# A graph network and a mixture of experts: the experts' second layer with tokens on partitions at once

## The chip, the cores and the metric

One core of a Trainium2 chip runs the whole kernel. The metric is device time in microseconds of one execution; lower is better.

## What is computed

The input is 16 graphs of 512 nodes with 128 features, and a 512 x 512 adjacency mask for each. The first block adds to every node the result of a small graph network; the second adds to every node a mixture of 8 experts, of which each node takes the best 2. Cut to what matters here:

```python
    # block 1, per graph: convolutions, message passing, GRU gates
    x = x + gnn(layernorm(x), adj)
    # block 2, on every node of every graph
    xn = layernorm(layernorm(x)) * gamma + beta
    logits = xn @ Wr + br                      # 8 experts
    top_vals, top_idx = top_k(logits, 2)
    w_full = softmax(top_vals) put at top_idx, 0 elsewhere
    for e in range(8):
        h = gelu(xn @ W1[e] + b1[e])           # 128 -> 256
        y_e = h @ W2[e] + b2[e]                # 256 -> 128
        y = y + y_e * w_full[..., e]
    x = x + y
```

## The kernel before, in words

Every engine runs one long list of instructions, written out by hand; semaphores join them. The order of these lists is what sets the order of the work.

**The graphs.** `iteration(g)` (one for each engine: TensorE L622, ScalarE L838, VectorE L1359, POOL L1001, the DMA queue SP L447) does the graph network of graph g, finishes graph d = g - 1 (residual sum, statistics, routing) and, from graph 4 on (`FIRST`), four expert tiles beside it. The products of the graph network are exact float32 from three passes in a reduced type (`product`, L527: high by high, low by high, high by low). Graph steps named in the prediction: `conv_sum` and `conv_diff` (the 17-tap convolution), `dist` (four products whose exponentials become the adjacency weights), the products with the hidden weights that begin with `HH + 1` (L687 to L691), the message product L706, the gates (L710 to L729), `nn` (L923) on ScalarE. `dist(3)` at L675 writes the PSUM bank M and so waits for `msg_done`, the copy `msg_t` on ScalarE (L882). Behind it on ScalarE come four exponentials (L885) and the gelu of tile 1.

**Routing and tiles.** Graphs 0 to 13 are routed: each normalized row goes by indirect DMA (POOL, `rows_to_experts`) to the region of its two experts in DRAM, with its weights for all 8 experts. A tile is 256 such rows of one expert. SP loads the rows (`xt`) and the expert's weights (`w_t`, one block per expert in DRAM: first layer high and low, second layer, biases, a one-hot row) through 8 buffers. The last two graphs are dense: all experts on all their rows, without routing. There are 66 tiles, 48 of them streamed beside graphs 4 to 15, and in the tail behind the graphs 18 tiles and 32 dense halves, in the order of `items` (L379).

**One tile.** TensorE turns the rows so that features lie on partitions (`turn`), ScalarE and VectorE split them into high and low (`turned`, `tile_lo`), TensorE makes the first layer (`hidden`), ScalarE the gelu (`gelu`). Then the part that is changed. `second` (L591) gives the result with features on partitions; `results` (L805) on ScalarE adds the bias, one value per partition, into `yT`; `back` (L600) turns it by two transposes so that tokens lie on partitions; `weigh` (L1303) on VectorE multiplies by each row's weight for the tile's expert; POOL adds the rows into `out` by indirect DMA (`add`, L970, and `last_add`, L989), each waiting until the adds before it have landed (in the tail: those of the experts before it). The row weight, `own_weight` (L1290), is made on VectorE: rows' weights times the one-hot row, then a sum. For a dense half `dense_weigh` (L1311) multiplies and adds into the graph's rows `x1_d` on VectorE.

**Where the tile steps stand.** TensorE: `tile_a(j)` (hidden of tile j, turn of the next, back of the one before) and `tile_b(j)` (second). ScalarE, in this order: results of the last tile of the graph before, `tile_gelu(0)`, `both` (L878), `tile_results(0)`, `msg_t`, the exponentials, `tile_gelu(1)`, `tile_turned(2)`, `normalized_rows` (L819), `tile_results(1)`, `xnT`, ..., `nm_h` (L908), `tile_results(2)`, `gap_weights` (L825, a tanh that VectorE's `place` waits for), the gates' tanh, ..., `nn`. VectorE: `operands_lo`, `residual_sum` with its statistics (L1397), `tile_own(0)` (L1398), the roots and tables of the routing, `tile_weigh(0)`, `normalize_x`, the four products with the mask (L1414), `tile_split(2)`, `tile_own(1)`, ..., `tile_split(3)`, `tile_own(2)`, `place`, ..., `tile_weigh(2)`, L1463, `tile_own(3)`, ..., `tile_weigh(3)`, `differences`.

**SP.** For each graph it stores the rows of graph d, loads `x_ln`, then `adj` of the next graph (L468, 1 MB, as soon as the mask products are done), `x_res`, and then, once the rows of the routing have landed, the four tiles of the next graph.

```python
                if g == FIRST - 1:
                    sp.wait_ge(w12_stored, 16)
                    sp.wait_ge(pads_stored, 16)
                if FIRST - 1 <= g < GRAPHS - 1:
                    chosen = [choice(g % 2, j) for j in range(SLOTS)]
                    for i in range(2):
                        sp.wait_ge(rows_out[i], 16 * NT * TOP * ((g - i) // 2))
                    for j in range(SLOTS):
                        next_loads(j)
```

## Time and profile before

| | |
|---|---|
| median of 3 runs | 658.0 us (655.03 to 658.53) |
| the profiled execution | 653.8 us, its span 652.0 us |
| TensorE busy | 614.0 us (94%) |
| TensorE loading weights (beside it) | 530.6 us (81%) |
| VectorE busy | 499.2 us (77%) |
| ScalarE busy | 418.1 us (64%) |
| POOL busy | 359.1 us (55%) |
| mean granted clock of TensorE | 0.985 |

The span is the time from the first to the last instruction; what the run's time has beyond it lies around the program. Busy shares are means over the whole span. A matmul in full float32 appears as two records, each with a weight load of its own; a busy time counts a record until its result is out, so records overlap, and the chain of waits shows their true distance. The chain of waits follows the work that ended last backwards, from each step to what released it; an idle time of an engine comes with the event that ended it.

### The profile page before, as it was taken

The numbers are of one execution on the slowest core, as the hardware profiler recorded it, in microseconds if no ns is written. First come the engines' busy times: TensorE is split into PE (matmuls) and PEld (weight loads), VectorE is DVE, ScalarE is ACT, GpSimd is POOL, SyncE is SP. The second block draws the span as 40 slices with busy tenths as digits, with TensorE's granted clock in tenths as the row PEclk, the third lists the DMA queues.
The fourth block names the chain that finished last, engine by engine and source line by source line (L and its number), as shares of the span: only waits on it lengthen the run. The fifth ranks groups of instructions, "written<-read, shape, count | busy, mean of one in ns | idle before, by whom it ended". The sixth has DMA issues, their size and how long they took to land.

```text
span 652.0 us, 12860 instructions
## 1 busy us (share of the span) xinstructions
PE 614.0 (94%) x3784; PEld 530.6 (81%) x3784; DVE 499.2 (77%) x2050; ACT 418.1 (64%) x824; POOL 359.1 (55%) x274
## 2 busy tenths in 40 slices
PE   2899999989999999999999999999999978999994
PEld 2779788777989897988888888888897957899993
DVE  6968898988888888888889888988787864544331
ACT  3644646494858575858586767676685745677772
POOL 3200405244854566575758685858485854545676
PEclk9998999999999999999999999999999998899998
DMA  8427241628398746465565655565647676993353
GB/s 299 145 80 266 73 123 53 204 89 247 65 291 250 191 115 186 128 165 153 138 171 141 165 149 161 153 166 144 165 110 192 167 167 157 236 252 46 53 94 46
DMA packets 93413, 101.01 MB, mean 155 GB/s; under 512 B 7664, under 2 KB 71920, under 8 KB 93040
## 3 DMA queue, kind: packets, MB, share of 16 engines
q1 hardware_dynamic: 70752, 83.27, 40.0%
q0 software_dynamic: 22592, 16.92, 17.0%
q8 instruction: 31, 0.51, 0.3%
q14 instruction: 38, 0.31, 0.2%
HBM read 75.85 MB, written 30.51 MB: 163 GB/s over the span
## 4 chain that ended last, share of the span: by engine, by line
PE 66%; DMA 7%; issue 7%; POOL 6%; ACT 6%; DVE 5%; POOLq 1%; another core or an unknown queue 0%; SPq 0%; DVEq 0%; ACTq 0%
PE G L706 9%; PE C L528 7%; PE C L530 7%; PE C L529 7%; POOL out L997 5%; PE G L528 5%; PE Y L596 5%; PE G L530 5%; PE G L529 5%; DMA out<-adj,ids 4%; PE M L534 2%; PE C L700 2%; PE Y L604 2%; DMA out<-ex,ids 2%; PE G L559 2%
## 5 line engine op out<-in xcount | busy, mean ns | idle before, releaser
L976 POOL DMA_INDIRECT out<-y_t,xt x96 | 159.4, 1660 | 121.7 <-DMA out<-y_t,xt 82.0
L1011 POOL DMA_INDIRECT routed<-row,at_u x112 | 130.6, 1166 | 116.2 <-DVE at_u L1208 83.6
L528 PE MATMUL C<-cv_h,w_hi 128*128 128x256 f32 (+1 forms) x432 | 131.6, 305 | 2.7 <-ACT tz L878 1.3
L530 PE MATMUL C<-cv_h,w_lo 128*128 128x256 f32 (+1 forms) x432 | 125.0, 289 | 0.0
L529 PE MATMUL C<-cv_l,w_hi 128*128 128x256 f32 (+1 forms) x432 | 124.9, 289 | 0.0
L528 PEld LDWEIGHTS C<-cv_h,w_hi 128*128 128x128 f32 x432 | 83.3, 193 | 5.7 <-issue 2.5
L529 PEld LDWEIGHTS C<-cv_l,w_hi 128*128 128x128 f32 x432 | 83.1, 192 | 1.3
L530 PEld LDWEIGHTS C<-cv_h,w_lo 128*128 128x128 f32 x432 | 83.0, 192 | 0.6
L596 PE MATMUL Y<-ge,w_t 128*128 128x256 f32 x228 | 59.8, 385 | 2.1 <-ACT ge L801 1.3
L706 PE MATMUL G<-ex,msg_t 128*128 128x512 f32 x128 | 58.9, 603 | 0.3 <-ACT gh L899 0.3
L596 PEld LDWEIGHTS Y<-ge,w_t 128*128 128x128 f32 x228 | 41.3, 192 | 12.7 <-issue 6.7
L801 ACT ACTIVATE ge<-H,w_t 128x256 f32<-128x256 f32 x114 | 47.9, 473 | 3.6 <-PE H L573 2.7
L908 ACT CAST cv_h<-G 128x512 fp32r<-128x512 f32 x16 | 9.4, 588 | 51.4 <-PE G L706 41.6
L706 PEld LDWEIGHTS G<-ex,msg_t 128*128 128x128 f32 x128 | 23.1, 190 | 23.5 <-issue 23.0
L528 PE MATMUL G<-xlT_h,w_hi 128*128 128x512 f32 x96 | 40.0, 417 | 1.5 <-DVE xlT_l L1139 1.5
L1414 DVE TENSOR_TENSOR ex<-ex,adj 128x512 f32<-128x512 f32 x64 | 39.8, 679 | 0.0
L530 PE MATMUL G<-xlT_h,w_lo 128*128 128x512 f32 x96 | 38.6, 402 | 0.0
L529 PE MATMUL G<-xlT_l,w_hi 128*128 128x512 f32 x96 | 38.3, 399 | 0.0
L571 PE MATMUL H<-xT_h,w_t 128*128 128x256 f32 x114 | 36.9, 323 | 0.0
L604 PE MATMUL Y<-cst,yT 128*128 128x128 f32 x146 | 29.9, 287 | 5.6 <-ACT yT L809 4.1
L1287 DVE TENSOR_TENSOR xT_l<-H,xT_h 128x256 fp32r<-128x256 f32 x57 | 23.9, 418 | 12.0 <-ACT xT_h L794 9.4
L809 ACT ACTIVATE yT<-Y,w_t 128x256 f32<-128x256 f32 x57 | 27.0, 474 | 9.3 <-PE Y L596 6.7
(264 smaller groups left out, 1703.3 us busy)
## 6 DMA issues: line engine op xcount, KB each, us to landing
w_t<-w_all SPq DMA_DIRECT2D x66, 392.0 KB, 3.5
adj<-adj_t SPq DMA_DIRECT2D x16, 1024.0 KB
xt<-routed SPq DMA_DIRECT2D x66, 144.0 KB
x_ln<-x SPq DMA_DIRECT2D x16, 256.0 KB
x_res<-x SPq DMA_DIRECT2D x16, 256.0 KB
wd<-w_all SPq DMA_DIRECT2D x10, 392.0 KB
out<-x SPq DMA_DIRECT2D x15, 256.0 KB
w_all<-w_s SPq DMA_DIRECT2D x1, 3136.0 KB, 11.4
```

The lines of the kernel that those rows point to most:

```text
L528: pe.matmul(psum, hi(w), rhs_h, start=start, stop=False)
L529: pe.matmul(psum, hi(w), rhs_l, start=False, stop=False)
L530: return pe.matmul(psum, lo(w), rhs_h, start=False, stop=stop)
L571: pe.matmul(half, w[:, h * P:(h + 1) * P], x_h, start=True, stop=False)
L596: last = pe.matmul(YO[bank_set(m)][:, 0:TILE], w[:, X_W2 + h * P:X_W2 + (h + 1) * P].bitcast(F32), ge[m % 2][:, h, :], start=(h == 0), sto ...
L604: last = pe.transpose(YO[bank_set(m)][:, TILE + t * P:TILE + (t + 1) * P], yT[m % 2][:, t * P:(t + 1) * P], ident)
L706: last = pe.matmul(G0[:], msg_t[:, j, :], ex[:, j, :], start=(j == 0), stop=(j == NT - 1))
L801: last = nc.scalar.activation(ge[m % 2][:, h, :], HID[bank_set(m)][:, h * TILE:(h + 1) * TILE], ACT.Gelu, bias=w[:, X_B1 + h:X_B1 + h + 1] ...
L976: nc.gpsimd.indirect_dma_start(out=out, out_offset=bass.IndirectOffsetOnAxis(ap=xt[j][:, t, R_ID:R_ID + 1].bitcast(U32), axis=0), in_=y_t[ ...
L997: nc.gpsimd.indirect_dma_start(out=out, out_offset=bass.IndirectOffsetOnAxis(ap=ids[:, i, t:t + 1], axis=0), in_=y_last[i][:, t, :], in_of ...
L1011: nc.gpsimd.indirect_dma_start(out=routed, out_offset=bass.IndirectOffsetOnAxis(ap=ats_u[d % 2][:, n:n + 1], axis=0), in_=rows[d % 2][:, n ...
L1414: nc.vector.tensor_tensor(ex[:, j, :], ex[:, j, :], adj[:, j, :], ALU.mult).then_inc(a_prod, 1)
```

## The change

The second layer swaps its operands: the activations of 128 tokens are the stationary operand and the weights stream, so tokens lie on partitions at once, in two halves of the PSUM bank. `results`, `back`, `yT` and their semaphores go. The bias now lies along the free axis: a block of 128 columns with `b2` on all 128 partitions is added to each expert's block in DRAM (`B2` in the host's weights, `X_B2` in the block), which grows from 784 to 912 columns. For a tile, ScalarE multiplies this block by each row's weight (`own_biases`, two activations, into `own_b`), and VectorE's `weigh` takes result times weight plus that, in two instructions. For a dense half VectorE adds weight times bias by two instructions of its own before it waits for the result. `tile_own(3)` moves ahead of `place` on VectorE.

```diff
             def second(m, w):
                 pe.wait_ge(gelu_done, m + 1)
                 if m > 0:
                     pe.wait_ge(y_done, m if m <= STREAMED else m - 1)
-                for h in range(HALVES):
-                    last = pe.matmul(YO[bank_set(m)][:, 0:TILE], w[:, X_W2 + h * P:X_W2 + (h + 1) * P].bitcast(F32),
-                                     ge[m % 2][:, h, :], start=(h == 0), stop=(h == HALVES - 1))
+                for t in range(TT):
+                    for h in range(HALVES):
+                        last = pe.matmul(YO[bank_set(m)][:, t * P:(t + 1) * P], ge[m % 2][:, h, t * P:(t + 1) * P],
+                                         w[:, X_W2 + h * P:X_W2 + (h + 1) * P].bitcast(F32), start=(h == 0),
+                                         stop=(h == HALVES - 1))
                 last.then_inc(pe_y, 1)
-            def back(m):
...
# ScalarE
-            def results(m, w):
-                act.wait_ge(pe_y, m + 1)
-                if m >= 2:
-                    act.wait_ge(pe_yT, m - 1)
-                nc.scalar.activation(yT[m % 2][:], YO[bank_set(m)][:, 0:TILE], ACT.Identity,
-                                     bias=w[:, X_B2:X_B2 + 1].bitcast(F32)).then_inc(yT_done, 1)
+            def own_biases(n, w, before=None):
+                act.wait_ge(own_done, n + 1)
+                if n >= 2:
+                    act.wait_ge(y_done, n - 1 if before is None else before + 1)
+                for t in range(TT):
+                    last = nc.scalar.activation(own_b[n % 2][:, t, :], w[:, X_B2:X_B2 + P].bitcast(F32), ACT.Copy,
+                                                scale=own_w[n % 4][:, t:t + 1])
+                last.then_inc(own_bias, 1)
...
-                tile_results(-1)
                 act.wait_ge(s_f32, g + 1)
...
                 nc.scalar.activation(both, C2[:, 0:HALF], ACT.Identity, scale=dv[:, D_SC2:D_SC2 + 1],
                                      bias=dv[:, D_BI2:D_BI2 + 1]).then_inc(both_f32, 1)
-                tile_results(0)
+                tile_bias(0)
                 act.wait_ge(pe_msgT, g + 1)
                 nc.scalar.copy(flat(msg_t), M[:]).then_inc(msg_done, 1)
...
                     normalized_rows(d)
-                tile_results(1)
+                tile_bias(1)
...
                 nc.scalar.copy(nm_h, G0[:]).then_inc(nmp_hi, 1)
-                tile_results(2)
+                tile_bias(2)
                 if tail:
                     gap_weights(d)
...
                 tile_turned(4)
+                tile_bias(3)
                 act.wait_ge(gate_step, 2 * g + 2)
                 nc.scalar.activation(nn[:], tr[:], ACT.Tanh, bias=vec[:, V_IH + 2:V_IH + 3]).then_inc(n_tanh, 1)
...
# VectorE
             def weigh(n, m=None):
...
-                dve.wait_ge(pe_yT, m + 1)
-                dve.wait_ge(own_done, n + 1)
-                nc.vector.tensor_tensor(y, YO[bank_set(m)][:, TILE:2 * TILE].rearrange("p (t d) -> p t d", t=TT),
-                                        over(own_w[n % 4][:], 2, [P, TT, P]), ALU.mult).then_inc(y_done, 1)
+                dve.wait_ge(pe_y, m + 1)
+                dve.wait_ge(own_bias, n + 1)
+                for t in range(TT):
+                    last = nc.vector.scalar_tensor_tensor(
+                        out=y[:, t, :], in0=YO[bank_set(m)][:, t * P:(t + 1) * P], scalar=own_w[n % 4][:, t:t + 1],
+                        in1=own_b[n % 2][:, t, :], op0=ALU.mult, op1=ALU.add)
+                last.then_inc(y_done, 1)
...
             def dense_weigh(m, q, e, u, k, before):
...
-                dve.wait_ge(pe_yT, m + 1)
...
+                for t in tiles:
                     last = nc.vector.scalar_tensor_tensor(
+                        out=x1_d[q][:, t, :], in0=wd[k % DENSE_BUFFERS][:, X_B2:X_B2 + P].bitcast(F32),
+                        scalar=w_d[q][:, t, e:e + 1], in1=x1_d[q][:, t, :], op0=ALU.mult, op1=ALU.add)
+                last.then_inc(dense_bias, 1)
+                dve.wait_ge(dense_bias, dense_before(m) + 1)
+                dve.wait_ge(pe_y, m + 1)
...
                 tile_split(3)
                 tile_own(2)
+                tile_own(3)
                 if tail:
                     place()
...
                 tile_split(4)
-                tile_own(3)
                 dve.wait_ge(n_tanh, g + 1)
...
# SP
             def dense_loads(k):
                 if k >= DENSE_BUFFERS:
-                    sp.wait_ge(pe_y, last_of_load(k - DENSE_BUFFERS) + 1)
-                    sp.wait_ge(yT_done, last_of_load(k - DENSE_BUFFERS) + 1)
+                    sp.wait_ge(y_done, last_of_load(k - DENSE_BUFFERS) + 1)
```

`last_loads` waits for `own_bias` of the tile that had the buffer, where it waited for `yT_done`. At the start SP loads one block more (0.5 MB), and the copy of `b2` into the expert blocks on VectorE goes.

## Rows read from the trace of the kernel before

**Rows 1.** Busy time by stage; behind the length: each engine, clock, DMA share, GB/s.
```profile
135.00:531.40 396.40, 391.93 (x2446) 338.40 (x2447) 338.64 (x1443) 272.61 (x529) 257.20 (x179) 1.00 0.60 161
531.40:652.00 120.60, 104.05 (x659) 93.59 (x657) 49.10 (x206) 74.25 (x176) 69.28 (x60) 0.93 0.60 132
```

**Rows 2.** Chain of waits through one streamed graph: start us, us, what.
```profile
297.32 0.25 PE C L530
...
300.86 0.44 PE Y L604 x2
...
308.39 0.23 PE M L559
308.62 0.12 PE H L571
...
313.35 0.86 PE Y L596 x4
...
317.10 0.23 PE G L528
...
319.17 0.22 PE Y L604 x2
319.38 0.79 PE C L700 x8
```

**Rows 3.** Timeline of ScalarE in the same graph: start us, us, what.
```profile
304.99 0.57 ACT L878 ACTIVATE tz<-C,dv 128x256 f32<-128x256 f32 x1 [0.33 <-issue]
305.86 0.47 ACT L809 ACTIVATE yT<-Y,w_t 128x256 f32<-128x256 f32 x1 [0.30 <-PE Y L596]
306.29 0.59 ACT L882 COPY msg_t<-M 128x512 f32<-128x512 f32 x1
...
311.57 0.84 ACT L801 ACTIVATE ge<-H,w_t 128x256 f32<-128x256 f32 x2
...
312.55 1.66 ACT L819 ACTIVATE row<-x,nb,rs 128x128 f32<-128x128 f32 x4
```

**Rows 4.** Timeline of VectorE in the same graph.
```profile
294.36 0.69 DVE L1451 SCALAR_TENSOR_TENSOR tr<-tr,gh 128x512 f32<-128x512 f32 x1 [0.52 <-ACT tr L913]
...
297.59 0.69 DVE L1463 TENSOR_TENSOR tr<-tr,C 128x512 f32<-128x512 f32 x1 [0.64 <-PE C L530]
...
301.34 0.42 DVE L1308 TENSOR_TENSOR y_t<-Y,own_w 128x256 f32<-128x256 f32 x1 [0.85 <-PE Y L604]
...
308.51 0.17 DVE L1297 TENSOR_REDUCE own_w<-pick_w 128x2 f32<-128x16 f32 x1
...
311.73 0.41 DVE L1308 TENSOR_TENSOR y_t<-Y,own_w 128x256 f32<-128x256 f32 x1
...
316.03 0.17 DVE L1297 TENSOR_REDUCE own_w<-pick_w 128x2 f32<-128x16 f32 x1
```

**Rows 5.** Timeline of VectorE in the tail.
```profile
584.82 0.61 DVE L1321 SCALAR_TENSOR_TENSOR x_d<-Y,w_d,x_d 128x128 f32<-128x128 f32 x2 [1.52 <-PE Y L604]
```

**Rows 6.** Timelines of SP, POOL and VectorE: a load, adds, a result.
```profile
315.60 0.37 SPq L468 DMA_DIRECT2D adj<-adj_t  x1
...
324.56 1.62 POOL L976 DMA_INDIRECT out<-y_t,xt  x1 [1.76 <-DMA out<-y_t,xt]
...
446.82 0.42 DVE L1308 TENSOR_TENSOR y_t<-Y,own_w 128x256 f32<-128x256 f32 x1 [0.29 <-remote]
...
460.25 1.62 POOL L976 DMA_INDIRECT out<-y_t,xt  x1 [2.26 <-DMA out<-y_t,xt]
...
554.64 1.56 POOL L997 DMA_INDIRECT out<-adj,ids  x1 [0.45 <-issue]
```

**Rows 7.** TensorE behind two waits, and windows of 1 us behind the second.
```profile
448.26 1.13 PE L596 MATMUL Y<-ge,w_t 128*128 128x256 f32 x4 [1.32 <-ACT ge L801]
...
554.82 0.69 PE L604 MATMUL Y<-cst,yT 128*128 128x128 f32 x2 [2.54 <-ACT yT L809]
...
555.00:556.00 1.00, 1.00 (x4) 0.91 (x4) 0.90 (x5) 0.77 (x3) 1.00 (x1) 0.50 0.94 195
```

More of the change, by code:

```diff
@@ L69 @@
 W2 = W1 + 16
-BLOCKS = W2 + 16
+B2 = W2 + 16
+BLOCKS = B2 + EXPERTS
 WCOLS = BLOCKS * P
@@ L97 @@
 X_W2 = 4 * P
-X_B1 = X_W2 + 2 * P
-X_B2 = X_B1 + HALVES
-X_OH = X_B2 + 1
+X_B2 = X_W2 + 2 * P
+X_B1 = X_B2 + P
+X_OH = X_B1 + HALVES
 XCOLS = X_B1 + 16
@@ L174, in gnn_moe @@
         w_t = [sb(f"w_t{i}", [P, XCOLS], F32R) for i in range(RING)]
-        yT = [sb(f"yT{i}", [P, TILE]) for i in range(2)]
+        own_b = [sb(f"own_b{i}", [P, TT, P]) for i in range(2)]
         y_t = [sb(f"y_t{i}", [P, TT, P]) for i in range(RING)]
@@ L333, in gnn_moe @@
         w_in = [sem(f"w_in{i}") for i in range(RING)]
-        pe_xtT, xT_hi, xT_split, pe_h, gelu_done, pe_y, yT_done, pe_yT, own_step, own_done, y_done, added = map(
-            sem, ("pe_xtT", "xT_hi", "xT_split", "pe_h", "gelu_done", "pe_y", "yT_done", "pe_yT", "own_step",
-                  "own_done", "y_done", "added"))
+        pe_xtT, xT_hi, xT_split, pe_h, gelu_done, pe_y, own_step, own_done, own_bias, dense_bias, y_done, added = map(
+            sem, ("pe_xtT", "xT_hi", "xT_split", "pe_h", "gelu_done", "pe_y", "own_step", "own_done", "own_bias",
+                  "dense_bias", "y_done", "added"))
         def hi(block, width=P):
@@ L389, in is_tile, with dense_before @@
             return len(item) == 4
+        def dense_before(m):
+            return sum(1 for item in items if not is_tile(item) and item[0] < m)
         def last_of_load(k):
@@ L424, in _ @@
                          weights[:, W2 * P:(W2 + 16) * P].rearrange("p (e h) -> p e h", e=EXPERTS)).then_inc(w2_loaded, 16)
+            sp.dma_start(w_s[:, :, X_B2:X_B2 + P].bitcast(F32),
+                         weights[:, B2 * P:(B2 + EXPERTS) * P].rearrange("p (e h) -> p e h", e=EXPERTS)).then_inc(
+                             w2_loaded, 16)
             sp.dma_start(routed[DUMMY:DUMMY + TAKEN, :], pads[0:TAKEN, :]).then_inc(pads_stored, 16)
@@ L629, in tile_a @@
                         turn(*tile_of(g, j + 1))
-                    if moe and not is_graph(tile_of(g, j)[0], 0):
-                        back(tile_of(g, j)[0] - 1)
                 def tile_b(j):
@@ L745, in _ @@
             g = GRAPHS - 1
-            back(STREAMED - 1)
             pe.wait_ge(nmp_split, GRAPHS)
@@ L750, in _ @@
             pe.wait_ge(z_tanh, GRAPHS)
-            for i in range(-2, len(items) + 1):
+            for i in range(-2, len(items)):
                 if i + 2 < len(items) and is_tile(items[i + 2]):
@@ L760, in _ @@
                         dense_hidden(*items[i + 1])
-                if 0 <= i - 1:
-                    back(items[i - 1][0])
                 if 0 <= i < len(items):
@@ L849, in tile_gelu, with tile_bias @@
                         gelu(n, w_t[slot])
-                def tile_results(j):
-                    n = tile_of(g, 0)[0] + j
-                    if moe and n >= 0:
-                        results(n, w_t[n % RING])
+                def tile_bias(j):
+                    if moe:
+                        n, slot, loads = tile_of(g, j)
+                        own_biases(n, w_t[slot])
                 act.wait_ge(pe_s, g + 1)
@@ L935, in _ @@
             d = GRAPHS - 1
-            results(STREAMED - 1, w_t[(STREAMED - 1) % RING])
             for i in range(-2, len(items)):
@@ L948, in _ @@
                         gelu(item[0], wd[item[4] % DENSE_BUFFERS])
-                if i >= 0:
-                    item = items[i]
-                    results(item[0], w_t[item[2]] if is_tile(item) else wd[item[4] % DENSE_BUFFERS])
+                if i >= 0 and is_tile(items[i]):
+                    m, n, j, loads = items[i]
+                    own_biases(n, w_t[j], number[n - 2] if n - 2 in number else n - 2)
                 if i == AT_SUM + 2:
@@ L1317, in dense_weigh @@
                     dve.wait_ge(y_done, before + 1)
-                dve.wait_ge(pe_yT, m + 1)
-                for i in range(TT):
-                    t = u * TT + i
+                dve.wait_ge(wd_in[k % DENSE_BUFFERS], 16 * (k // DENSE_BUFFERS + 1))
+                tiles = range(u * TT, (u + 1) * TT)
+                for t in tiles:
                     last = nc.vector.scalar_tensor_tensor(
-                        out=x1_d[q][:, t, :], in0=YO[bank_set(m)][:, TILE + i * P:TILE + (i + 1) * P],
+                        out=x1_d[q][:, t, :], in0=wd[k % DENSE_BUFFERS][:, X_B2:X_B2 + P].bitcast(F32),
[3 more added lines that the diff above has]
+                dve.wait_ge(pe_y, m + 1)
+                for i, t in enumerate(tiles):
+                    last = nc.vector.scalar_tensor_tensor(
+                        out=x1_d[q][:, t, :], in0=YO[bank_set(m)][:, i * P:(i + 1) * P],
                         scalar=w_d[q][:, t, e:e + 1], in1=x1_d[q][:, t, :], op0=ALU.mult, op1=ALU.add)
@@ L1586 @@
             put(W2 + 2 * n + h, e["W2"][n][half, :])
+        put(B2 + n, np.broadcast_to(e["b2"][n], (P, P)))
     v = np.zeros((P, VCOLS), np.float32)
```

17 lines of the change are left out of this document (5 added, 12 removed).

## The prediction

> **What bounds the kernel now.** I read the windows by stage first. From 135.0 to 531.4 us (the graphs that carry expert tiles, 12 of them) TensorE is busy for 391.93 of 396.40 us; in the tail behind them it is busy for 104.05 of 120.60 [rows 1]. So the streamed stage looks like a TensorE program with no air in it. Then the chain of waits through one streamed graph: pieces of TensorE follow one another, and once per graph the chain leaves it: the gates of a graph end at 297.57, VectorE and ScalarE work, and the turning back of the last tile starts at 300.86 and takes 0.44 where the pair takes 0.22 when nothing is late [rows 2]. A graph lasts 33.4 us.
>
> The tail is another matter. The chain there is POOL's: its adds into `out` begin for the last 18 tiles at 554.64 [rows 6] and run, each run of an expert waiting for the landing of the one before, to the end. They lag the results: in the streamed graphs a result written at 311.73 [rows 4] is added at 324.56, one written at 446.82 at 460.25 [rows 6], 12.8 and 13.4 us late. The second pair stands behind a graph in which TensorE had lost over a microsecond (1.32 us idle [rows 7]), and POOL did not use that to catch up. I take it that POOL is held by the large loads: the 1 MB load of `adj` is issued at 315.60, and the adds that lie behind it wait for landings (1.76 and 2.26 us before the two adds shown [rows 6]). POOL would then move with the loads, 9 us behind each.
>
> **The change, part by part.** The program order decides: ScalarE, VectorE and TensorE each run a written list.
>
> (a) Turning back goes: 0.22 us of TensorE per tile [rows 2], 4 per graph, and the wait before the first, together about 0.55 us there (0.44, and 0.1 that TensorE stood before it). Alone that is 0.55 + 3 x 0.22 = 1.2 us per graph.
>
> (b) The second layer becomes 8 records of 128 columns for 4 of 256. Today's four take 0.86 us, 0.215 each. Half the columns is 0.108; a record with 8 columns, all weight load, takes 0.79/8 = 0.099. If load and stream overlap, the tile stays at 0.86; if they add, it is 8 x (0.108 + 0.099) = 1.65, so 0.79 more. A first layer record of 256 columns, its own load included, takes 0.12 [rows 2], hardly more than a load alone: they overlap. I take 0.92 us, +0.06. In a sentence by itself: the Trainium skill ("TensorE: Matmul & The Clock Gate", Back-to-back issue gap) has about 81 ns per matmul in a stream of load and matmul pairs at 128 columns where the isolated gap is 56, a ratio which, as an estimate, would make the tile 1.24 us and the whole 8 us slower than my sum; no row before shows this shape.
>
> (c) ScalarE loses one activation per tile (`yT`: 305.86 to the next start 0.43 later) and gets two of 128x128 with a scale per row. Four such take 1.66 us [rows 3], so the pair 0.78. None for dense items. Its work is not the point; its place is. The new `tile_bias(0)` stands where `tile_results(0)` stood, behind `both` (304.99, 0.57 long) and ahead of `msg_t` at 306.29 [rows 3]. It waits for the tile's own weight. VectorE makes that in `tile_own(0)`, behind the residual sum and its statistics: the reduce ends at 308.51 + 0.17 = 308.68 [rows 4]. The change moves only `tile_own(3)`. So ScalarE, free at 305.56, stands for 3 us.
>
> Step by step, on the clock of this graph. VectorE drops its 0.85 us wait ahead of the last weighing [rows 4], but ScalarE's `xT_h` copy allows only 0.36 of that (one `yT`, less overlap), so the weight is there at 308.32. Bias pair to 309.13 (the next instruction's start). `msg_t` starts there, not at 306.29: +2.84. Behind it ScalarE is back to back, table load, four `exp`, table load, `gelu(1)`, so `gelu(1)` starts at 311.57 + 2.84 = 314.41 and ends 0.84 later, 315.25 [rows 3]. TensorE: `dist(3)` waits for `msg_t`, 309.13 + 0.59 + 0.03 = 309.75, where it started at 308.39 and now could at 307.84: 1.9 us idle. From `dist(3)` to `second(1)` is 313.35 - 308.39 = 4.96, less a turning back 4.74, so 314.49; `gelu(1)` ends at 315.25: 0.8 us idle. `second(1)` at 315.27 instead of 313.35, so the product at 317.10 starts at 319.02 [rows 2]: +1.92. From there to the gates' end two turnings back are gone: +1.92 - 0.44 = +1.48, and two second layers at +0.06: **+1.6 us per graph**, 19 us over 12 graphs.
>
> (d) The other three. `tile_bias(1)` waits for the weight of 316.03 + 0.17 = 316.20 [rows 4], but ScalarE comes to it only at 312.55 + 2.84 + 1.56 = 316.95: nothing, and `xnT` behind it is done 0.6 us before TensorE wants it. `tile_bias(2)` waits and then holds the small tanh of the gap for about 1 us, on which VectorE's routing waits. Behind that lie VectorE's waits for ScalarE and TensorE, 0.52 and 0.64 us [rows 4], which cover it; uncovered it would be up to 1 us per graph. `tile_bias(3)` lies before `nn`, where ScalarE waits for VectorE anyway: nothing.
>
> (e) VectorE weighs with two instructions: a pair of that kind takes 0.61 against 0.42 [rows 4, 5], 0.2 more per tile. It is in the sum for `tile_weigh(0)` (hidden: ScalarE's `exp` is later). In the tail a dense item has four for two, 1.2 us of VectorE where an item lasts 1.9: hidden. The dense loads wait for `y_done` now, three buffers deep: hidden.
>
> (f) 64 KB more per weight load, 16%: four per graph, on the queue that POOL's landings wait behind; and 0.5 MB at the start, off every chain. Bound: nothing to 0.8 us per graph where POOL runs free. I take 1 us in all.
>
> (g) The end. POOL is last, not TensorE, so what counts is when POOL's chain starts to run free: behind the last load of `adj`, in the 11th of the 12 graphs, with 10 graphs' delay ahead of it. 10 x 1.6 + 1 = 17 us. The tail saves TensorE some 50 x 0.22 = 11 us and its waits; it ends ahead of POOL by more than before, so that saving is worth nothing.
>
> Sum, against this profile's own time of 653.8 (span 652.0 and 1.8 around): 653.8 + 17 = 670.8. The median of the three runs is 4.2 above that execution, so 675.0 us.
>
> **The rivals.**
> *The bias never waits.* If the own weight came before 305.56, TensorE would win (a) alone, 1.2 x 12 = 14 us, and what POOL follows of it would end the kernel: between 644 and 658, say 650. It decides at that point, and the row says the weight is 3 us late. Chance 0.09.
> *It nets out.* Gain and wait cancel, or POOL takes most of the wait up: within 0.5%. 0.05.
> *POOL catches up.* Its lag could shrink by 10 us before results bind it; the end then moves by 19 - 10 = 9: 667. The steady lag speaks against it, the waits for landings inside its chain, which more time between results would swallow, for it. 0.20.
> *The clock falls.* The 1.9 us of idle per graph could cost the granted clock. Idle 1.32 us did not; 2.54 us did, and at 555 to 556 us it was 0.50, the level of 1.2 GHz [rows 7]. Three microseconds at half clock, partly under the 0.8 us of idle, give 1 to 2 us more per graph: about 690. 0.12.
> *Load and stream add* in the second layer: 0.79 - 0.06 on two tiles of the path, 1.5 x 10: 690. 0.06. The ratio of the Trainium skill (above) would give 683 and lies between this and my term.
>
> **How the numbers follow.** The forecast has what is left, 0.48, own range 668 to 681. The range down to 660 takes in POOL catching up with a smaller wait, and up to 693 most of the clock and load cases. Half a per cent is about what a measurement of this kernel can tell from no change: faster 0.09, same 0.05, slower 0.86.
>
> **What would show it.** In a streamed graph of the changed kernel: ScalarE idle about 2.8 us ahead of the first bias activation, released by VectorE's reduce of the own weight; TensorE idle near 1.9 us at the fourth `dist` product and 0.8 us before the second tile's second layer; a period of 35.0 us; 0.11 to 0.12 us per second layer record; the gap from result to add still about 11 us. If ScalarE doesn't wait at `tile_bias(0)`, or the period is under 33.4, the forecast is wrong at its root; if the period is 35 and the end comes at 667 or less, POOL's hold was misread; records of 0.2 us would put (b) wrong.

## The result, and the profile after

The changed kernel takes 677.1 us (median of 4 runs, 674.2 to 680.6) where the kernel before takes 658.3 beside it: a ratio of 1.033, 95% interval 1.028 to 1.038. The forecast was 675.0 in a range of 660 to 693. The profiled execution took 676.15, its span is 674.3 at a mean clock of 0.981.

| | before | after |
|---|---|---|
| profiled execution, span, us | 653.8, 652.0 | 676.15, 674.3 |
| first streamed result (`y_t` of tile 0) | 143.31 | 147.48 |
| result of tile 4, of tile 44 | 177.20, 514.69 | 182.55, 537.26 |
| so one graph, mean of these ten | 33.75 | 35.47 |
| last streamed result (tile 47) | 534.26 | 558.05 |
| first add of the tail, us | 554.64 | 575.84 |

The start is 4.2 us later, the ten graphs lose 17.2 (1.72 each), and the last result is 23.8 later. Behind it the tail is as long as it was: 652.0 - 534.3 = 117.7 us before, 674.3 - 558.1 = 116.2 after.

The windows come first, over the same ten graphs, of the kernel before and then of the kernel after (columns as in [rows 1]: length; busy time of TensorE, its weight loads, VectorE, ScalarE, POOL; granted clock; DMA share; GB/s).

```profile
177.20:514.69 337.49, 334.81 (x2103) 289.93 (x2102) 290.24 (x1234) 233.66 (x454) 221.75 (x155) 1.00 0.62 167
```

```profile
182.55:537.26 354.71, 330.09 (x2188) 286.90 (x2187) 297.16 (x1274) 241.74 (x495) 224.62 (x158) 1.00 0.62 167
```

TensorE is busy for 330.1 us where it was busy for 334.8, and stands for 24.6 us where it stood for 2.7: 21.9 us more of standing less 4.7 us of work are the 17.2 us. The granted clock stayed at 1.00 in both, the level of 2.4 GHz.

Next the waits of the kernel after: engine, result and line, what it waited for; us in total, times, longest.

```profile
ACT own_b L808 <- DVE own_w L1296: 43.4, 21, 3.3
PE M L566 <- ACT msg_t L881: 13.1, 9, 1.7
PE Y L605 <- ACT ge L798: 8.8, 12, 1.7
```

ScalarE waits 43 us for own weights, a wait that the kernel before does not have, and TensorE has the two waits that the prediction named: for `msg_t` and for the gelu. In ten of the twelve streamed graphs the wait ahead of `tile_bias(0)` is 3.3 us long, in the other two 2.05 and 1.59. One graph of ScalarE's timeline (start, duration, engine, line, operation; in brackets the idle time before it and its releaser) answers to [rows 3]:

```profile
317.06 0.56 ACT L877 ACTIVATE tz<-C,dv 128x256 f32<-128x256 f32 x1 [0.17 <-issue]
320.94 0.69 ACT L808 ACTIVATE own_b<-w_t,own_w 128x128 f32<-128x128 f32 x2 [3.31 <-DVE own_w L1296]
321.54 0.56 ACT L881 COPY msg_t<-M 128x512 f32<-128x512 f32 x1
326.95 0.84 ACT L798 ACTIVATE ge<-H,w_t 128x256 f32<-128x256 f32 x2
```

The same graph on VectorE, which answers to [rows 4]:

```profile
318.40 0.69 DVE L1348 SCALAR_TENSOR_TENSOR x<-G,x_res 128x512 f32<-128x512 f32 x1
319.12 0.87 DVE L1083 BATCH_NORM_STATS2 st<-x 128x6 f32<-128x128 f32 x4
320.74 0.17 DVE L1296 TENSOR_REDUCE own_w<-pick_w 128x2 f32<-128x16 f32 x1
324.64 0.60 DVE L1308 SCALAR_TENSOR_TENSOR y_t<-Y,own_w,own_b 128x128 f32<-128x128 f32 x2
```

The reduce ends at 320.91, and ScalarE's bias pair starts at 320.94. TensorE, same graph:

```profile
319.62 0.85 PE L566 MATMUL G<-v_s,u_s 128*128 128x512 f32 x3
322.15 0.50 PE L566 MATMUL M<-v_s,u_s 128*128 128x512 f32 x1 [1.68 <-ACT msg_t L881]
327.84 1.16 PE L605 MATMUL Y<-w_t,ge 128*128 128x128 f32 x8 [0.70 <-ACT ge L798]
```

Three of the four `dist` products run, the fourth stands 1.68 us for `msg_t`, and `second(1)` 0.70 for the gelu. On the chain of waits the second layer of a tile (8 records) weighs 0.89 us, 0.11 each. Last, the loads of the page, of the kernel after (median us from issue to landing at the end):

```profile
w_t<-w_all SPq DMA_DIRECT2D x66, 456.0 KB, 5.0
w_all<-w_s SPq DMA_DIRECT2D x1, 3648.0 KB, 12.6
```

The page of the kernel before has 392.0 KB with 3.5 us, and 3136.0 KB with 11.4.

### The profile page after: what moved, and what is told of

Same layout as the page of the kernel before. It is cut to its first block, busy times and chain, and to the rows that moved or that the text cites. A ratio compares the mean times of both kernels' runs of the same rounds, so it can differ in the third digit from the quotient of the medians.

```text
span 674.3 us, 13409 instructions
## 1 busy us (share of the span) xinstructions
PE 598.5 (89%) x3980; PEld 523.1 (78%) x3980; DVE 527.8 (78%) x2179; ACT 414.1 (61%) x858; POOL 360.6 (53%) x274
## 3 DMA queue, kind: packets, MB, share of 16 engines
q0 software_dynamic: 22592, 16.92, 16.8%
## 4 chain that ended last, share of the span: by engine, by line
PE 50%; DVE 17%; ACT 16%; issue 10%; POOL 3%; DMA 2%; another core or an unknown queue 1%; POOLq 0%; SPq 0%; DVEq 0%; ACTq 0%
PE G L706 8%; PE Y L605 6%; PE G L535 5%; PE G L537 4%; PE G L536 4%; PE C L537 3%; PE C L535 3%; PE C L536 3%; ACT ex L884 3%; DVE v_s L1071 2%; POOL out L996 2%; PE G L605 2%; DVE st L1083 2%; ACT L798 2%; ACT ge L798 2%
## 5 line engine op out<-in xcount | busy, mean ns | idle before, releaser
L975 POOL DMA_INDIRECT out<-y_t,xt x96 | 171.5, 1786 | 132.1 <-DMA out<-y_t,xt 79.2
L1010 POOL DMA_INDIRECT routed<-row,at_u x112 | 119.7, 1069 | 125.1 <-DVE at_u L1207 92.5
L535 PE MATMUL C<-cv_h,w_hi 128*128 128x256 f32 (+1 forms) x432 | 130.1, 301 | 4.6 <-issue 2.7
L808 ACT ACTIVATE own_b<-w_t,own_w 128x128 f32<-128x128 f32 x132 | 45.8, 399 | 53.3 <-DVE own_w L1296 43.4
L605 PEld LDWEIGHTS Y<-w_t,ge 128*128 128x128 f32 x456 | 57.9, 193 | 21.3 <-ACT ge L798 11.7
L605 PE MATMUL Y<-w_t,ge 128*128 128x128 f32 x456 | 62.3, 280 | 11.1 <-ACT ge L798 8.8
L578 PE MATMUL H<-xT_h,w_t 128*128 128x256 f32 x114 | 34.5, 303 | 1.5 <-DVE xT_l L1286 1.5
L580 PE MATMUL H<-xT_h,w_t 128*128 128x256 f32 x114 | 32.2, 283 | 0.0
```

Source lines behind the costliest of these rows:

```text
L535: pe.matmul(psum, hi(w), rhs_h, start=start, stop=False)
L578: pe.matmul(half, w[:, h * P:(h + 1) * P], x_h, start=True, stop=False)
L580: last = pe.matmul(half, w[:, (2 + h) * P:(3 + h) * P], x_h, start=False, stop=True)
L605: last = pe.matmul(YO[bank_set(m)][:, t * P:(t + 1) * P], ge[m % 2][:, h, t * P:(t + 1) * P], w[:, X_W2 + h * P:X_W2 + (h + 1) * P].bitcas ...
L808: last = nc.scalar.activation(own_b[n % 2][:, t, :], w[:, X_B2:X_B2 + P].bitcast(F32), ACT.Copy, scale=own_w[n % 4][:, t:t + 1])
L975: nc.gpsimd.indirect_dma_start(out=out, out_offset=bass.IndirectOffsetOnAxis(ap=xt[j][:, t, R_ID:R_ID + 1].bitcast(U32), axis=0), in_=y_t[ ...
```

## The experiments

Below, "one graph" is always (result of tile 44 - result of tile 4) / 10 of the profiled execution, 33.75 in the kernel before. Ratios are against the kernel before on the same chip.

### The wait alone

`before_wait` is the kernel before, with the wait put ahead of its own bias:

```diff
+                if moe:
+                    act.wait_ge(own_done, tile_of(g, 0)[0] + 1)
                 tile_results(0)
```

> The kernel before, with nothing but a wait added on ScalarE: ahead of the results of tile 0 it waits for that tile's own weight. No second layer, bias or load is changed. Theory: period 33.4 + about 1.9 = 35.2 us or a little more (yT is late too, for the second turning back), time 658 + 17 to 23 = 675 to 681. Rival (the new second layer, the extra VectorE work or the loads make the loss): 658 to 661.

Measured: ratio 1.033 (1.028 to 1.037), 35.89 us per graph. Two of its waits:

```profile
ACT yT L809 <- DVE own_w L1299: 37.6, 12, 3.9
PE M L559 <- ACT msg_t L884: 14.6, 11, 2.0
```

So ScalarE's place behind the own weight is enough for a loss as large as the change's, with no other part of it present. That the two ratios are equal is in part chance: `before_wait` still turns back and loses 2.14 us per graph where the change loses 1.72, and its tail is 108.9 us long where the change's is 116.2 (POOL, which is only 1.5 us behind the first result of each graph, ends before TensorE and VectorE there).

### The weight earlier

`own0_first` is the change with the own weight of tile 0 made first:

```diff
+                tile_own(0)
                 tile_split(1)
                 operands_lo(g)
 ...
                     residual_sum(d, G0)
-                tile_own(0)
```

> Only the own weight of tile 0 is made earlier: VectorE's first work of each graph's list. Theory (ScalarE's wait at the first bias costs TensorE 1.9 us): the 3.31 us wait is gone, and the second one takes its place: the bias of tile 1 waits for its weight, which VectorE makes behind the mask products, xnT is late by about 1 us and TensorE waits for it. Graph period 33.3 us for 35.2 in the changed kernel, time 677 - 10 x 1.9 = about 658. Rival (the loss is VectorE's longer list or the heavier loads, the wait only a symptom): period stays near 35, time 675 or more.

`own01_first` moves `tile_own(1)` there too.

> The own weights of tiles 0 and 1 both first in VectorE's list. Theory: neither bias waits, TensorE gets what the turning back cost it: period 32.2 to 32.5 us, time 646 to 652 if POOL follows the adj loads, which come earlier. If POOL cannot run faster than a graph in 33 us, its lag grows and the time stays at 655 to 658. Rival (VectorE's list or loads): period near 35.

Measured: `own0_first` 1.029 (1.019 to 1.038), `own01_first` 1.027 (1.019 to 1.034). Both expectations missed: 658 us was expected of the first and 646 to 652, or 655 to 658, of the second; 673.3 and 667.6 came, and the mean graph is 35.19 and 34.77 us. The wait did go: ScalarE's for own weights falls from 43.4 us to 17.7 and 15.1 (in `own01_first` what is left is 1.4 us, once per graph, at tile 2), TensorE's at `dist(3)` in `own01_first` from about 1.7 us per graph to 1.1 us in all. The total hardly moved, but the graphs say why. In `own01_first` the first results stand 33.6, 32.0 and 32.3 us apart, as fast as the prediction's part (a) would have it; in `own0_first` 33.1, 33.2, 33.7 and 32.9. Then both have one graph of 40 us (a slip, as I call it below), and the later ones take 33.1 to 37.6. This is the place, in `own01_first`, on TensorE:

```profile
265.48 0.69 PE L546 MATMUL H<-cst,xt 128*128 128x128 f32 x2 [5.72 <-DMA xt<-routed]
265.81 0.77 PE L535 MATMUL C<-xc_h,w_hi 128*128 128x512 f32 x1
266.39 0.63 PE L536 MATMUL C<-xc_l,w_hi 128*128 128x512 f32 x1
```

TensorE waits 5.72 us for the rows of the next graph's first tile. Behind the wait a product of 512 columns takes 0.63 us by its record; where the clock is full it is 0.39 to 0.40, and the granted clock from 265 to 269 us is 0.50, the level of 1.2 GHz. So the slip costs the wait and some microseconds at half clock behind it (the prediction's rival on the clock, in another place). The rows are late because SP issued their load at 262.81, once POOL's scattered rows had landed, and this is POOL, SP and VectorE ahead of it, `own01_first`:

```profile
244.37 3.72 POOL L975 DMA_INDIRECT out<-y_t,xt  x1 [0.30 <-issue]
254.74 1.61 POOL L975 DMA_INDIRECT out<-y_t,xt  x1 [4.08 <-DMA out<-y_t,xt]
```

```profile
245.03 0.38 SPq L472 DMA_DIRECT2D x_ln<-x  x1
246.67 0.37 SPq L475 DMA_DIRECT2D adj<-adj_t  x1
262.81 0.39 SPq L437 DMA_DIRECT2D xt<-routed  x1
```

```profile
244.16 2.48 DVE L1423 TENSOR_TENSOR ex<-ex,adj 128x512 f32<-128x512 f32 x4
```

An add that is usually 1.6 us long takes 3.72 here; the next add, which waits for it to land, starts at 254.74, over 10 us behind the start of the first. The 1 MB load of the mask is issued 2.3 us behind the long add's start, but it is not what makes it long: an add of 1.6 us would have ended 0.7 us before the load was issued. What lies over the add is VectorE's four products with the mask, from 244.16 to 246.64. The load follows them because SP waits for them. `no_adj` (below), in which no mask is reloaded, has the long add too, over the same products; POOL and VectorE:

```profile
148.02 2.72 POOL L975 DMA_INDIRECT out<-y_t,xt  x1 [0.30 <-issue]
```

```profile
146.81 2.49 DVE L1422 TENSOR_TENSOR ex<-ex,adj 128x512 f32<-128x512 f32 x4
```

In the 14 traces of this case all 66 of these adds that take more than 2.6 us start inside those products, or up to 0.2 us ahead of them, and end 1.43 to 1.51 us behind their end. So POOL's add is held while the products run. The place that answers to it in the kernel before, with VectorE last:

```profile
277.05 1.57 POOL L976 DMA_INDIRECT out<-y_t,xt  x1 [0.30 <-issue]
...
281.80 1.61 POOL L976 DMA_INDIRECT out<-y_t,xt  x1 [0.30 <-issue]
```

```profile
281.88 0.37 SPq L468 DMA_DIRECT2D adj<-adj_t  x1
...
290.12 0.38 SPq L429 DMA_DIRECT2D xt<-routed  x1
```

```profile
279.36 2.49 DVE L1414 TENSOR_TENSOR ex<-ex,adj 128x512 f32<-128x512 f32 x4
```

The products start behind the end of the add, the next add goes without a wait, and the rows' load is issued at 290.12. With a faster TensorE the products come earlier against POOL's adds.

A held add alone does not make a slip. The kernel after has ten of 2.7 to 3.8 us and TensorE waits for no rows longer than 0.6 us; the kernel before has one of 3.80 us at 178.73, and its next add starts 4.1 us behind it without a wait. The seven graphs of 39 us or more, in six kernels, have more in common: the held add is the second of its pair, two scatters follow, the next pair waits 3.8 to 4.2 us for the landing, and two more scatters of rows stand behind it, so the rows' load is issued 15.4 to 16.8 us behind the mask's load (5.6 to 10.4 in all other graphs). Whether the mask's load makes that landing later is not shown.

### The wider loads alone

`before_wide` is the kernel before with 128 unused columns in every expert's block, and 0.5 MB more loaded at the start:

```diff
-BLOCKS = W2 + 16
+BLOCKS = W2 + 16 + EXPERTS
-XCOLS = X_B1 + 16
+X_DEAD = X_B1 + 16
+XCOLS = X_DEAD + P
```

> The kernel before with expert blocks of 912 columns instead of 784, 128 of them dead, and the extra load of 0.5 MB at the start. In the changed kernel the first streamed result came 4.2 us later than before, which no wait of ScalarE explains. If the heavier loads at the start do that: first result near 147 us for 143.3, period unchanged at 33.4 to 33.6, time 658 + 2 to 5. If it was the clock's phase in that one run: 658 to 659.

Measured: ratio 1.025 (1.018 to 1.031), 34.58 us per graph; all in graphs of 32.6 to 35.3 but one of 40.15, in which TensorE waits 4.49 us for the rows. There an add at 385.44 takes 2.78 us, over the mask products of 384.30 to 386.78. So the wider blocks cost 2.5% in the kernel before, against the "1 us in all" of my part (f). In the profile most of it is the slip: the other nine graphs take 33.96 us in the mean, and the first result is 2.4 us later. How wider blocks lead to a slip is not shown. `after_narrow` asks whether they cost it in the changed kernel too. It reads one resident bias block (expert 0's) for every tile, so the choice of the bias by the expert is left out:

```diff
-X_B2 = X_W2 + 2 * P
-X_B1 = X_B2 + P
+X_B1 = X_W2 + 2 * P
 ...
-                    last = nc.scalar.activation(own_b[n % 2][:, t, :], w[:, X_B2:X_B2 + P].bitcast(F32), ACT.Copy,
+                    last = nc.scalar.activation(own_b[n % 2][:, t, :], b2_any[:], ACT.Copy,
```

> The changed kernel with blocks of 784 columns: the bias of all tiles is read from one resident block (expert 0's), so the choice of the bias by the expert is left out; order, waits and instruction counts of the change stay. Theory (in the changed kernel ScalarE's wait sets the period and hides what the wider loads cost): the period stays at 35.1 to 35.3 us and the ratio against the kernel before at 1.027 to 1.038. Rival (the loads cost their 2.5% of before_wide in the changed kernel too, or own01_narrow's 1.3%): period 34.6 or less, ratio 1.01 to 1.02.

Measured: ratio 1.027 (1.020 to 1.035), 35.16 us per graph. The wait stays (30.6 us of ScalarE for own weights, 13.1 of TensorE for `msg_t`), and so does the loss: narrowing gives 0.3 us per graph, and the intervals of the two ratios overlap. The two causes are not a sum. Where ScalarE's wait has slowed the graphs to 35 us, the kernel after has no wait for rows above 0.6 us; that it is the slower pace which keeps the slip away is argued, not shown.

`own01_narrow` is `own01_first` with the same narrow blocks (784 columns for 912; the 896 of the expectation is wrong).

> own01_first with blocks of 784 columns in place of 896: the bias of all tiles is read from one resident block (expert 0's), so the choice of the bias by the expert is left out, and everything else is as in own01_first (two bias activations per tile, two weighing instructions, own weights of tiles 0 and 1 made first). It prices the wider loads where ScalarE's wait is nearly gone. If the loads are what gave own01_first's gain back (graphs of 32.0 to 32.3 us, then one of 40.3 and others of 33 to 35), the periods stay at 32.0 to 32.7, the graph of 40 is gone or shrinks to 36, the first result comes at 143 to 145 us, and the ratio against the kernel before is 0.975 to 0.995. If VectorE's order (own weights first, everything else 0.5 us later) or POOL gives it back, the graph of 40 stays and the ratio is 1.01 to 1.027, within 0.5% of own01_first's own start gain of 3 to 4 us.

Measured: ratio 1.014 (1.004 to 1.023); one graph of 39.9 us stays, the later ones take 34.5 to 35.6. So narrow loads do not take the slip away; the ratio is 1.3% lower than that of `own01_first`, between intervals that still overlap. In the last five graphs `msg_t` waits 1.1 to 2.5 us each, mostly for something that the profile does not name, and TensorE 6.7 us in all for the gelu: this order of VectorE's list is not free either. What sets it was not settled.

### What holds the tail

`tail_light` is the change with one of three first-layer passes in the 32 dense halves (the low products are left out, some 15 us of TensorE), `no_adj` the change without the reloads of the mask (all graphs use graph 0's).

> The changed kernel, with the dense halves' first layer in one pass instead of three: the two products with a low part are left out, 32 x 0.48 = 15 us of TensorE in the tail. Theory (POOL's chain of adds sets the end): TensorE ends some 15 us earlier, time within 0.5% of the changed kernel (674 to 680). Rival (TensorE's tail bounds too): 662 to 668.

> The changed kernel without the reloads of the mask: graph 0's mask serves all graphs, 15 loads of 1 MB are left out. Theory (POOL is held by those loads): the lag from a result to its add falls from 11 to 13 us to 6 or less, the period stays at 35.2, the end comes up to 8 us earlier (668 to 674). Rival (POOL's own instructions and landings set the lag): lag stays at 10 us or more, time within 2 us of the changed kernel.

```diff
-                        hidden_products(HID[bank_set(m)], wd[...], xd_h[q][:, cols], xd_l[q][:, cols])
+                        hidden_products(HID[bank_set(m)], wd[...], xd_h[q][:, cols], xd_l[q][:, cols], low=False)
 ...
-                    sp.dma_start(adj[:], adj_v[g + 1]).then_inc(adj_loaded, 16)
+                    pass
```

Measured, two runs each: 1.032 (1.016 to 1.049) and 1.033 (1.012 to 1.055), the change's own ratio. 15 us would be 2.3%, so TensorE's products of the dense halves have slack, as (g) has it: the tail is 114.1 us, 2.1 shorter for 15 us less of them. But my reading of what holds POOL's lag is not borne out: the lag from the result of a graph's first tile to its add is 5.2 us, steady, in `no_adj` and in `tail_light`, which has all its mask loads, while it is 11.7 to 12.3 in the change and 1.5 in `before_wait`. It has several levels at which it stays. The tail does not follow it from 12 to 5 us of lag (116.2 us in the change, 116.0 in `no_adj`); only at 1.5 is it shorter, 108.9. In all other kernels it is 114 to 119 us.

### A turned layer with nothing on ScalarE

`bias_pe`, from the kernel before: the layer turned, its bias added by TensorE in one product, 784 columns as before, one weighing instruction.

```diff
+                pe.matmul(YO[bank_set(m)][:, 0:TILE], w[:, X_B2:X_B2 + 1].broadcast_to([P, P]),
+                          ident_r[:].unsqueeze(1).broadcast_to([P, TT, P]), start=True, stop=False)
+                for t in range(TT):
+                    for h in range(HALVES):
+                        last = pe.matmul(YO[bank_set(m)][:, t * P:(t + 1) * P], ge[m % 2][:, h, t * P:(t + 1) * P],
+                                         w[:, X_W2 + h * P:X_W2 + (h + 1) * P].bitcast(F32), start=False, ...)
```

> From the kernel before: the second layer is turned as in the change (tokens on partitions), but its bias is added by TensorE, one 256-column product per tile whose stationary operand is the bias column repeated and whose moving operand is the identity repeated. ScalarE gets nothing (it loses the activation into yT), nothing of the experts' path waits for the own weight before the weighing, the loads keep their 784 columns, and VectorE weighs with one instruction as before. My theory (the loss is ScalarE's place behind the own weight, the turned layer itself is worth what it removes): no wait of ScalarE for VectorE at the message step, TensorE spends 0.89 + 0.12 us per tile where it spent 0.86 + 0.22, and the period of a streamed graph falls from 33.4 to 32.4 to 33.0 us; over 12 graphs that is 5 to 12 us, if POOL and the loads keep up, so a ratio of 0.980 to 0.992 against the kernel before. The rival that the turned layer costs by itself (a layer of 128-column records disturbs what follows) says 33.4 or more and a ratio of 1.00 or above. The rival that loads and POOL bound the kernel as soon as TensorE is quicker says: period 32.7 at first, then one graph of 38 to 40 us with TensorE waiting for the rows of the next tile, and a ratio within 0.5% of 1.

`bias_early` issues the bias product ahead of the wait for the gelu; `no_bias` leaves the bias out.

```diff
-                pe.wait_ge(gelu_done, m + 1)
                 if m > 0:
                     pe.wait_ge(y_done, m if m <= STREAMED else m - 1)
                 pe.matmul(YO[bank_set(m)][:, 0:TILE], w[:, X_B2:X_B2 + 1].broadcast_to([P, P]), ...)
+                pe.wait_ge(gelu_done, m + 1)
```

> bias_pe with its bias product issued ahead of the wait for the gelu, so that it runs in the time in which TensorE would stand (in bias_pe TensorE stands 7.9 us ahead of that product over ten graphs, 4.2 of it for the gelu, and the product costs 0.12 to 0.5 us each). Theory (TensorE is the bound again in bias_pe, with 0.12 to 0.5 us per tile of bias and some 0.8 us of waits per graph): the period falls from 33.4 to 33.0 us, 4 to 6 us in all, ratio to the kernel before 0.995 to 1.005. Rival (ScalarE's gelu sets that point, and whatever TensorE saves ahead of it is waited out): period 33.3 to 33.4, ratio 1.005 to 1.01 as bias_pe.

> bias_pe without its bias product: the output layer's bias is left out of every expert's result. It is the turned layer alone, with narrow loads, no activation for the results and one weighing instruction: the most that the turning could give. By the sum of the prediction (a turning back gone, 1.2 us per graph, layer time even) the period is 32.2 us and the end 12 us earlier, if POOL follows: ratio 0.980 to 0.990. If ScalarE's gelu (or the rows of the next tiles, as in own01_first) becomes the bound as soon as TensorE gains, the period is 32.8 to 33.4 with TensorE waiting 0.8 us or more per graph ahead of the second layer, and the ratio is 0.995 to 1.005.

| | us per graph | last streamed result | ratio (interval) |
|---|---|---|---|
| `bias_pe` | 34.03 | 541.97 | 1.008 (1.003 to 1.014) |
| `bias_early` | 33.24 | 528.83 | 1.009 (1.005 to 1.013) |
| `no_bias` | 34.33 | 541.07 | 1.010 (1.004 to 1.016) |

Most of the change's loss is gone, but none is faster, not even the one with less work on TensorE and nothing new anywhere: all three ratios are above what my theories gave (0.980 to 0.992, 0.995 to 1.005, 0.980 to 0.990); `bias_early`'s lies where its rival had it. `bias_pe` has no slip, so the rival with one graph of 38 to 40 us did not come true there. In it TensorE stands 7.9 us (in 340 us) ahead of the bias product; `bias_early` leaves 2.0 us of such waits (in 310 us), and its profile is 0.5 us per graph quicker than before's, yet its median is no better: one profile is one run of twelve. `no_bias` shows it best. Its results are 33.0, 32.5, 33.8 and 31.8 us apart, then 39.5, 33.9, 33.1, 31.9, and again 39.2: five of these nine are under 33.75, by up to 1.9 us, and two give it all back. At the first of the slow ones, `no_bias`, TensorE, POOL, SP in turn:

```profile
298.42 0.69 PE L538 MATMUL H<-cst,xt 128*128 128x128 f32 x2 [5.89 <-DMA xt<-routed]
```

```profile
276.98 3.96 POOL L944 DMA_INDIRECT out<-y_t,xt  x1 [0.30 <-issue]
...
287.45 1.61 POOL L944 DMA_INDIRECT out<-y_t,xt  x1 [3.93 <-DMA out<-y_t,xt]
...
293.06 1.24 POOL L979 DMA_INDIRECT routed<-row,at_u  x1 [0.30 <-issue]
```

```profile
279.53 0.37 SPq L468 DMA_DIRECT2D adj<-adj_t  x1
...
295.79 0.38 SPq L430 DMA_DIRECT2D xt<-routed  x1
```

The same picture as in `own01_first`: an add of 3.96 us over the mask products (277.02 to 279.50), the next add only at 287.45, the scatters behind it to 294.3, the rows' load at 295.79. The two slips alone are 12.7 us above two graphs of 33 us. A lower clock explains little of the rest: over the graphs without a slip the granted clock is 1.00 in `no_bias` and `bias_early`, and 0.99 over the ten graphs of `bias_pe`.

### POOL's order

`no_bias_order` moves two of POOL's four row scatters ahead of the second tile's add, into a wait; the bias is left out as in `no_bias`.

```diff
                 tile_add(0)
-                tile_add(1)
                 if tail and d < ROUTED:
                     pool.wait_ge(rt_step, router_first(d) + ROUTER_STEPS)
-                    rows_to_experts(d, 0, NT // 2)
+                    rows_to_experts(d, 0, NT // 4)
+                tile_add(1)
+                if tail and d < ROUTED:
+                    rows_to_experts(d, NT // 4, NT // 2)
```

> no_bias (the output layer's bias left out) with one thing moved on POOL: the first two of the four row scatters that stand behind the add of a graph's second tile go ahead of it, into the 5 us in which POOL waits for the landing of the add before (5.50 us in the kernel before at 333.56). Nothing else changes, and TensorE's, VectorE's and ScalarE's lists stay. Theory (POOL and what its landings release, the next graph's loads, are a second bound of 33.4 us per graph beside TensorE's 33.4; that is why a turned layer with no bias at all, with periods of 31.8 to 32.5 us between, gives all of it back in two graphs of 39 us whose TensorE waits for the rows): POOL's graph is 2.6 us shorter, the graphs of 39 us are gone or down to 35, the wait for the rows falls from 10 us to under 4, the last streamed result comes at 530 us or earlier and the ratio against the kernel before is 0.983 to 0.995. Rival (the rows come late by the DMA queues' own load, not by POOL's order): at least one graph of 38 us or more stays and the ratio is 1.00 to 1.015.

Measured: ratio 0.995 (0.990 to 1.000), against 1.010 (1.004 to 1.016) of `no_bias`: 1.5% from POOL's order alone. 33.20 us per graph, nine of ten at 32.1 to 33.3, last streamed result at 532.59. (The profiled execution took 653.0 us; the twelve lie between 643.0 and 655.3.) POOL in the kernel before:

```profile
333.56 1.78 POOL L976 DMA_INDIRECT out<-y_t,xt  x1 [5.50 <-DMA out<-y_t,xt]
```

and in `no_bias_order`:

```profile
334.04 0.99 POOL L979 DMA_INDIRECT routed<-row,at_u  x1 [0.30 <-DVE at_u L1178]
335.34 1.09 POOL L979 DMA_INDIRECT routed<-row,at_u  x1 [0.30 <-issue]
339.18 1.66 POOL L944 DMA_INDIRECT out<-y_t,xt  x1 [2.75 <-DMA out<-y_t,xt]
```

The wait for the landing is half as long, because scatters that must be made anyway fill it. Adds over the mask products it has as before, six of them above 2.6 us in the streamed graphs; only one leads to a slip. The theory holds in its main point, but not in full: one slow graph of 39 us stays, early (its add at 214.97 takes 4.02 us, over the mask products of 215.05 to 217.53), TensorE's waits for rows in the whole run are 7.7 us at the tile's turning, 10.6 in `no_bias`, not under 4, and the ratio is at the weak end of what was expected. A version that keeps the bias and beats the kernel before was not found; this order of POOL's with the bias kept was not tried.

## Why the prediction was right, step by step

**(a) and (b)** The turning back is gone, and the second layer takes 0.89 us for 0.86, where I took 0.92. Load and stream of 128-column records overlap: one after the other they would have taken 1.65 us by the prediction's own sum. The estimate of 1.24 us from the Trainium skill ("TensorE: Matmul & The Clock Gate", Back-to-back issue gap) does not fit this stream: 0.11 us per record is what the trace shows. (Its price in the prediction, 8 us and 683, counts 12 graphs where (g) counts 10: by (g)'s rule it is 6.)

**(c)** is what sets the period of the changed kernel, at the size given. ScalarE's wait: 3.31 us (forecast 3); TensorE idle 1.68 at `dist(3)` (1.9, because the bias pair holds ScalarE for 0.60 us and I took 0.8) and 0.70 at `second(1)` (0.8); graph of the rows shown 35.2, mean of ten 35.47 (35.0 from 33.4); loss per graph 1.72 (1.6). `before_wait` has the wait alone and a loss as large. But the wait is not the only thing that can cost this much: with it gone, `own01_first` is still 2.7% slower, `own01_narrow` 1.4%, by slips and waits that the prediction has no term for. The rival that the bias never waits falls with the 3.31 us, and so does that of load and stream adding up; the rival on the clock falls for the change itself, since 1.7 us of idle left the clock at 1.00.

**(d)** `tile_bias(2)` waits 1.38 us and no wait of TensorE follows from it in the profile. `tile_bias(3)` does not wait.

**(e)** The weighing pair takes 0.60, as forecast from the pair of [rows 5]. In the tail VectorE's four instructions are not wholly hidden: the chain of waits of the kernel after runs through them (a second layer of TensorE starts at 603.44 behind the pair that VectorE ends at 603.30), where that of the kernel before is POOL's and its landings' alone, from 599 us on at least. It made the tail no longer.

**(f)** is the term that was wrong as the prediction put it: "64 KB more per weight load ... I take 1 us in all". It measures 2.5% by itself in the kernel before, and between nothing and 3 us (0.3 per graph) in the changed one, where ScalarE's wait may cover it. The bound "0.8 us per graph where POOL runs free" is what `before_wide` shows (34.58 - 33.75 = 0.83), and it is mostly one slip. I should have asked what the loads cost if (c) were not there. I also held that the start load lay off every chain; the profile after is 4.2 us later at the first result. The load is not needed for that: kernels with narrow blocks start anywhere from 143.5 (`bias_early`) to 148.8 (`bias_pe`), and `tail_light`, with the wide blocks and the same start load, starts at 143.9. In these five it goes with the granted clock of the start, which from 20 to 100 us is 0.98 in `bias_early`, `tail_light` and the kernel before, 0.96 in the kernel after, 0.94 in `bias_pe`. So this part of the loss in the profile is not shown to be the change's.

**(g)** The end moved by 22.3 us of span, not 17: the ten graphs' 17.2 are as summed, and the 4.2 of the start were missing (the first streamed graph and the last tiles add 1.2 each, and the tail is 1.5 shorter). For the profiled execution the sum gave 670.8, and it took 676.15: 5.3 too low. The profile of before lay 4.2 under its median, that of after 0.9 under its own: 3.3 the other way. So the forecast of the median is only 2 us off because two errors offset, and that is luck. That POOL is last and TensorE's saving in the tail is worth nothing agrees with `tail_light`, but the chain of waits of the kernel after is POOL's alone only from 637.9 us on; before that it runs through TensorE and VectorE. That the mask's load holds its lag does not: the lag was 12 or 5 with the loads and 5 without, at the same time.

**The rival that it would be faster** (650 us) did not come true even with the wait gone. It priced TensorE's 1.2 us per graph as a gain, as if TensorE were the only bound. `no_bias` has that gain and nothing to pay, and it is 1.0% slower; with POOL's order changed as well it is 0.5% faster, at the edge of what can be told from no change.

## What to carry to other kernels

When an instruction moves to another engine's list, look first at what the new operand is made from and where its maker stands in its own list: here one wait of 3.3 us per graph, put alone into the kernel before, lost as much as the whole change did. When a kernel shows TensorE busy for 99% of a stage, count the other loop as well, the one through POOL, its landings and the next loads: it can be just as long, and then a saving on TensorE can be given back there: here it moved VectorE's products onto a POOL transfer whose landing others wait for. What helped was in that loop: independent transfers put between two that must wait for each other. And before a transfer that runs long is laid to the load issued beside it, look at what the other engines do at that time, and at a run without the load.

## What was not expected of the hardware

- An indirect add into DRAM takes 1.6 us of POOL, but up to 4.15 when VectorE's four mask products (2.5 us) lie over it: 66 adds above 2.6 us in 14 traces end 1.43 to 1.51 us behind the products' end, one of them in `no_adj` without the mask's load. One add that starts inside the products was not held (216.48 in `tail_light`, 1.91 us).
- Where such an add is the second of its pair, the pair that waits for its landing starts 9.4 to 10.5 us behind it (seven slips).
- Behind 5.7 to 5.9 us without work TensorE ran products of 512 columns at 0.63 us per record for 0.40, for about 5 us (298.42 to 303.2 in `no_bias`, granted clock 0.50); behind 1.7 us it did not (clock 1.00 in the kernel after). Behind 2.4 us it did once (492.38 in `own01_first`, clock 0.63 and 0.51 in the next 4 us) and once not (422.46, clock 1.00).
- The bias product of `bias_pe`, 256 columns with the bias column repeated as the stationary side, takes 0.28 us by its record in 71 of 98 cases, and 0.68 at one tile of each streamed graph; why there is not shown.
